# Cross half of a gated attention block on one core: statistics in slot 3, rest of the high part in slot 4, GpSimd's parts one slot on

## The reference, cut to what matters

```python
# x, ctx: 32 sequences x 128 positions x 128 features; 16 heads of 8 features
x = x + tanh(g_xattn) * attention(layernorm(x), ctx, ctx)      # cross half: keys = values = ctx
x = x + tanh(g_ffn) * ffn_block(layernorm(x), ...)             # on pairs of sequences, S = 128
# ffn_block: rotary embedding, projections q, k, v, causal attention, output projection,
#            layernorm, 8 experts with the two best gates, layernorm
```

## Time and profile before

| what | value |
|---|---|
| median of 3 executions | 498.08 us (497.17 to 498.41) |
| the profiled execution | 498.87 us |
| its span, first to last instruction | 497.1 us |
| PE busy | 437.8 us, 88% |
| DVE busy | 381.9 us, 77% |
| POOL busy | 326.3 us, 66% |
| ACT busy | 276.5 us, 56% |

### The profile page before, as it was taken

The page is one execution under the profiler, slowest core; times in us unless marked ns, Lnnn a source line. Parts: engine busy times, 40 slices in busy tenths (PEclk is TensorE's granted clock), DMA queues, the critical chain, the costliest instruction groups (busy, mean ns, idle before and its releaser), DMA issues.

```text
span 497.1 us, 15905 instructions
## 1 busy us (share of the span) xinstructions
PE 437.8 (88%) x5728; PEld 274.9 (55%) x5728; DVE 381.9 (77%) x1189; ACT 276.5 (56%) x693; POOL 326.3 (66%) x704
## 2 busy tenths in 40 slices
PE   0479888889888999999999999998799999999983
PEld 0245444545444666666666666665466666667552
DVE  5788999999877777777767676861568999999981
ACT  1136767676765666566566566666245545454540
POOL 5465767676689988788888877320327676767654
PEclk9999999999889999999999999999699999999995
DMA  7866785854633334443433444300000000000000
GB/s 163 188 157 156 191 186 137 190 136 109 152 94 94 91 86 114 113 99 89 103 86 90 104 101 121 87 11 6 1 0 12 23 11 23 16 19 22 13 21 21
DMA packets 88333, 42.70 MB, mean 86 GB/s; under 512 B 16312, under 2 KB 88128, under 8 KB 88256
## 3 DMA queue, kind: packets, MB, share of 16 engines
q1 hardware_dynamic: 77392, 38.93, 32.3%
q10 hardware_dynamic: 10864, 2.76, 2.6%
HBM read 5.75 MB, written 2.10 MB: 16 GB/s over the span
## 4 chain that ended last, share of the span: by engine, by line
PE 39%; DVE 29%; POOL 15%; issue 8%; ACT 4%; DMA 1%; ACTq 1%; SPq 1%; POOLq 0%; DVEq 0%
PE u_bank L432 8%; DVE nm L618 7%; PE s_bank L385 6%; PE s_bank L375 5%; DVE z_acc L949 5%; POOL xn_all L249 4%; PE t_bank L357 4%; PE u_bank L445 2%; PE s_bank L779 2%; PE u_bank L800 2%; DVE stats L574 2%; POOL rstd L244 2%; PE st_bank L779 2%; POOL rc L267 2%; POOL z_rstd_ L677 1%
## 5 line engine op out<-in xcount | busy, mean ns | idle before, releaser
L618 DVE TENSOR_REDUCE nm<-s_bank 128x4 f32<-128x512 f32 x256 | 173.3, 684 | 56.0 <-PE s_bank L385 55.4
L515 ACT ACTIVATE pt<-st_bank 128x512 f32<-128x512 f32 x256 | 151.2, 601 | 85.8 <-PE st_bank L385 44.2
L432 PE MATMUL u_bank<-pt,vaug 128*32 128x128 f32 x2048 | 110.9, 289 | 1.6 <-DVE ao L635 0.3
L385 PE MATMUL s_bank<-qk 64*128 64x128 bf16 x1024 | 102.4, 225 | 11.2 <-DVE nm L618 6.2
L385 PE MATMUL st_bank<-qk 64*128 64x128 bf16 x1024 | 102.5, 221 | 0.0
L385 PEld LDWEIGHTS s_bank<-qk 64*128 64x128 bf16 x1024 | 68.9, 97 | 38.9 <-issue 18.8
L385 PEld LDWEIGHTS st_bank<-qk 64*128 64x128 bf16 x1024 | 69.0, 95 | 0.4
L432 PEld LDWEIGHTS u_bank<-pt,vaug 128*32 128x32 f32 x2048 | 41.1, 109 | 29.6 <-issue 4.8
L375 PE MATMUL s_bank<-mqk,esel 64*128 64x256 bf16 x256 | 49.7, 274 | 0.6 <-DVE nm L618 0.4
L375 PE MATMUL st_bank<-mkq,esel 64*128 64x256 bf16 x256 | 49.7, 274 | 0.0
L291 POOL TENSOR_TENSOR part<-r,part 128x512 bf16<-128x512 f32 x32 | 37.1, 1159 | 2.6
(11 more groups left out here) (120 smaller groups left out, 884.0 us busy)
## 6 DMA issues: line engine op xcount, KB each, us to landing
qk<-part SPq DMA_DIRECT2D x221, 128.0 KB, 2.7
x_all<-x SPq DMA_DIRECT2D x16, 128.0 KB, 2.7
qk<-qrow SPq DMA_DIRECT2D x32, 64.0 KB, 2.2
qk<-mts ACTq DMA_DIRECT2D x64, 32.0 KB, 2.6
out<-z_o SPq DMA_DIRECT2D x16, 128.0 KB, 1.8
c_all<-ctx_in SPq DMA_DIRECT2D x14, 128.0 KB, 3.1
ewt<-exp_t SPq DMA_DIRECT2D x1, 512.0 KB
qk<-part ACTq DMA_DIRECT2D x3, 128.0 KB, 2.8
```

Source lines behind the costliest of these rows:

```text
L385: return pe.matmul(bank[:, j * P:(j + 1) * P], k if keys_first else q, q if keys_first else k, start=not masked, stop=True, skip_group_che ...
L432: ins = pe.matmul(u_bank[b][32 * j:32 * j + 32, r * P:(r + 1) * P], v, pt[m % 4][:, j, :], start=half == 0, stop=half == 1, skip_group_che ...
L515: act.activation(pt[m % 4][:, :, :].rearrange("k j q -> k (j q)"), st_bank[m % 2][:, :], ACT.Exp).then_inc(ex, 1)
L618: dve.tensor_reduce(nm[q % 2][:, first:first + HEADS], s_bank[n % 2][:, :].rearrange("q (j k) -> q j k", j=HEADS), AX_X, ALU.max, negate=T ...
```

## The change: two pairs change places in the cross half

On VectorE the statistics of unit `s+3` move from slot 4 to slot 3, and the rest of the high part of unit `s+2` from slot 3 to slot 4. On GpSimd, in cross units only, the middle part moves from slot 4 to 5, the low part from 5 to 6, the norm's factor from 5 to 4 and the permuted copy from 6 to 7. No instruction is added, removed or changed. The program text of PE, ACT and SP is the same.

```diff
                 if 0 <= s + 2 < UNITS:
-                    if t == (4 if in_x(s + 2) else 6):
+                    if t == (5 if in_x(s + 2) else 6):
                         middle_part(s + 2)
-                    if t == (5 if in_x(s + 2) else 7):
+                    if t == (6 if in_x(s + 2) else 7):
                         low_part(s + 2)
                 if in_x(s + 3):
-                    if t == 5:
+                    if t == 4:
                         normalised(s + 3)
-                    if t == 6:
+                    if t == 7:
                         permute_context(s + 3)
...
-                    if t == 3:
+                    if t == 4:
                         rest_of_high(s + 2)
-                if in_x(s + 3) and t == 4:
+                if in_x(s + 3) and t == 3:
                     statistics(s + 3)
```

## The result

The changed kernel takes 499.31 us (498.95 to 500.02, 7 runs), the kernel before 497.76 in the same comparison (497.17 to 498.93, 7 runs): ratio 1.003, interval 1.0018 to 1.0041, which is 1.55 us more. Two further comparisons gave 1.002 (1.0005 to 1.0036) and 1.0029 (1.0015 to 1.0042). The forecast was 498.0 with "the same" at 0.71. The time lies in the range 496.0 to 499.9, but all three intervals exclude no change, and the forecast of no difference was wrong.

The account below looks back on a forecast made before the run. Cross units were taken as bound by GpSimd's loop, unit 13 by SP's DMA queue. Start-up -1.3 and units +0.4 reach unit 13 0.9 us earlier, lost waiting there: sum 0, 498.0 us, range 496.0 to 499.9.

Parts of the forecast that it names:

- the same: Whole kernel: time between 496.6 and 499.6 us, no difference one measurement can tell; chance 0.71.
- +0.05 us a unit: Steady cross units: GpSimd's later result makes PE wait, cancelling VectorE's 0.37 us gain; bounds -0.37 to +0.37.
- about +0.4 over eight units: Cross half: the added time per steady unit, taken over eight units, about +0.4 us.
- Closes a loop of 8.4 us: Steady cross unit: GpSimd's work and its wait for `ao` form a loop, so VectorE's 0.37 us gain has no way out.
- Start-up, -1.3: Start-up: unit 2's `xp` gets its factor early, so all that follows comes 1.3 us sooner; bounds 0 to -2.0.
- SP's queue sets unit 13: End of cross half: SP's DMA queue keeps unit 13's stack landing at 130.22 us, change 0.0; forecast case, chance 58%.
- the sum of 0: Whole kernel: PE reaches unit 13 0.9 us earlier but waits that much longer for its DMA, net 0.
- 76.26 plus a fixed sum of DMA issues: Unit 13's start: set by SP issuing without pause from 76.26 us, however fast VectorE is.
- the prediction's own sign of being wrong: Changed kernel's profile: unit 13 without a DMA wait would mean SP was no bound.
- The copy beside `xp`: Slot 0 of cross units: GpSimd's later copy overlapping VectorE's `xp` costs 0, bounded by 0.37 us; blocking rival 10%.
- The rule weighed in the prediction: VectorE and GpSimd share ports, the second to issue blocked; any overlap paid, up to 0.37 us more a unit.
- a third low clock stretch: PE's clock falls once more because PE idles longer: +0.7 to +1.3 us, 499.0 us; chance 12%.

Follow-up runs that it names:

- both edits: Against the changed kernel, GpSimd's low part back in slot 5, ahead of line 312's addition, and the permuted copy in slot 2: 498.30 us, ratio 0.9998.
- half the cast: Against the kernel with both edits, ACT's cast of the high part made for only half its columns in units 2 to 15: 497.82 us.
- one engine's part alone: Two kernels against the kernel before: only VectorE's part of the change, 508.27 us, or only GpSimd's part, 508.11 us.
- the second profile: Profile of the unedited kernel before, submitted against itself: 498.74 against 497.77 us, ratio 1.0016.
- start-up alone: Against the kernel before, the change made only in steps below 0, on both engines: 496.88 us, ratio 0.9984, again 496.88 us, 0.9978.
- the low part in slot 5: Against the changed kernel, only GpSimd's low part moved back to slot 5, ahead of line 312's addition: 497.88 us, ratio 0.9998 to the kernel before.
- later steps alone: Against the kernel before, the change made only from step 0 on, with the old start-up: 500.96 us, ratio 1.0058.

## Why the prediction was wrong

*The failed step: "+0.05 us a unit", "about +0.4 over eight units".* The mechanism was right: VectorE's wait has no way out, GpSimd closes the loop at line 312, PE waits for line 308. The size was not: the steady unit is 8.58 and not 8.38 to 8.43, so 0.20 a unit and 1.8 us over nine units, four times the term. The loop can be followed in the changed kernel's rows from one transposition (line 440) to the next:

```profile
88.40 0.23 PE L440 MATMUL m_bank<-idb,mst 128*128 128x128 bf16 x1
...
91.55 0.44 PE L445 MATMUL u_bank<-idf,us 128*128 128x128 f32 x2 [0.41 <-ACT us L531]
...
92.10 0.22 PE L385 MATMUL s_bank<-qk 64*128 64x128 bf16 x1
```

PE, held by ACT's `us`, ends the sixth scores at 92.32; VectorE's maxima start at 92.35 and `ao` ends at 93.59, 5.19 us after the transposition began. Then 0.09 to the addition, 3.27 of GpSimd without a pause to 96.95, and 0.05 to PE: 8.60. The prediction had 3.2 to 3.3 for GpSimd, which is right. What it had wrong is `ao`. Before, it ended 86.29 - 80.88 = 5.41 us after the transposition began, and I took it 0.37 earlier, 5.04. It came 0.22 earlier, for once VectorE's own wait is gone, the sixth maxima wait for PE. Even with GpSimd freed (both edits) it comes at 5.15. The term was a small difference of large sums, and an error of 0.15 in one of them made it four times as large. With 0.20 for 0.05 in the prediction's own sum, SP would have stood at 77.0 instead of 76.3 and the forecast, by estimate, at 498.8.

*"Closes a loop of 8.4 us"* was half of the matter. In the kernel before three ways are close to 8.4: the one over VectorE (the trace's chain), the one over ACT's `us` (which holds 8.38 with both edits, and 8.17 with half the cast), and GpSimd's right beneath. So relieving VectorE or GpSimd brought nothing, while GpSimd's added time came through for the most part, as one engine's part alone shows at 0.8 and 0.98.

*Start-up, -1.3:* right in mechanism and nearly in size: 1.34 between the two profiles, 1.14 when each is counted from its own first `xp`. Unit 0's first maxima stand at +0.6 (17.57 for 16.96; +0.8 from the first `xp`) where +0.7 was said. By itself the start-up is worth 1.0 us at the end.

*"SP's queue sets unit 13":* wrong as a fixed part of the kernel, and the second step that failed, since the sum of 0 rested on it. I read one execution, and "76.26 plus a fixed sum of DMA issues" isn't fixed: SP was through 2.1 us earlier in the second profile. That profile and all three of the changed kernel have no wait at unit 13, the prediction's own sign of being wrong. The wait comes and goes: start-up alone has it in one profile of two, the low part in slot 5 has it too. From unit 12 to 16 the two profiles of the kernel before take the same time with it and without it.

*The copy beside `xp`:* 0 was right for the changed kernel, whose `xp` takes 0.68, though the copy runs on for 0.2 us after `xp` has started. Where the copy starts 0.1 to 0.4 us after `xp`, in one engine's part alone, `xp` pays 0.30 to 0.48, so the two engines do meet there without a semaphore between them. The rule weighed in the prediction (the Trainium skill, SBUF — State Buffer, "Who interferes with whom") agrees with those rows in that `xp` pays; that any overlap is paid is not what the rows of the changed kernel show.

*Clock.* At like clock the changed kernel is slower by 1.0 us in the high group (498.74, four runs, against 497.75) and by 0.75 in the low one (499.78 against 499.03). The change's two parts add up to about that: start-up alone -1.0 and -1.2, later steps alone +2.2 (one run) and +1.8, together +1.2 and +0.6. The places of unit 12 give +0.5 of it, with 0.9 between the two profiles of the kernel before; what the rest is stays open. Of the full 1.2 to 1.5 us some 0.5 would be the share of low clock: 4 of the changed kernel's 24 runs in the two later comparisons are in the high group, against 53 of 98 before, with 1.3 us between the groups. But the kernel before, compared with itself, had 3 of 12 there, so it isn't shown that the change moves the share. In three profiles of the changed kernel the low stretch ahead of the experts lasts 13.7, 10.2 and 13.7 us, in two of before 10.2 both times; no run here moved the low stretches alone. The rival "a third low clock stretch", at 12%, comes nearest to this part.

## What to carry to other kernels

A wait that an engine shows inside a loop is no gain until the loop that sets the period is found: shorten or free each candidate alone (here a move of one slot, or half a cast) and see which moves the period. When several loops are nearly equally long, as three are here, price an added wait in full, because it is paid in every round, and a gain at nothing until all of them are shorter. Split a reordering by time as well as by engine: what helps in the start-up can be had without what it costs later.

Read a term like "this DMA wait bounds the stage" from two executions before a forecast rests on it.

## What the runs showed that I had not expected

- Low clock comes at the change from cross to self half, beginning between 129 and 140 us (147 to 148 where one engine's part alone had made the cross half longer), in stretches of about 3.4 or 6.8 us, whether PE waits 1.43 us for a DMA there or not. Before the experts they are 10.2 or 13.7 us long. A last one begins between 484 and 490 us (495 to 496 for one engine's part alone) and lasts to the end of the kernel. The kernel's own scatter goes with the mean clock: 497.75 at high and 499.03 at low.
- An overlap of 0.2 us between GpSimd's copy and VectorE's two-part `xp` leaves `xp` at 0.68 and costs GpSimd's next operation 0.07. A copy that starts 0.1 us after `xp` costs `xp` 0.30 and itself 0.12; one that starts 0.4 us after it costs `xp` 0.48 and itself 0.04.
- The same kernel against itself came out at 1.0016 with an interval that excludes 1.
